# Layer 2's product table in a four-layer graph network: one fp32r pass over stacked parts in place of fp32 matmuls

## The reference, cut to what matters

```python
h = h + segment_sum(basis[:, s, None] * x_j, row * 25 + idx[:, s], n * 25)   # s in 0..3
out = einsum('nki,kio->no', h.reshape(n, 25, 32), weight)
out = out / clip(deg, 1.0)[:, None]
out = out + x @ root_weight + bias
```

## Time and profile before

| what | value |
|---|---|
| median of 3 runs | 12156.67 us (12153.4 to 12159.37) |
| the profiled execution's own time | 12152.8 us |
| its span in the profile | 12150.8 us |
| mean granted TensorE clock over the span | 0.954 |
| stretch in which the table is made | 2984.58 us (first transpose) to 3170.68 us (first gather from Y) |

### The profile page before, as it was taken

How to read it: one execution, slowest core, us unless ns; L and a number is a source line. 1 busy time by engine, 2 the same in 40 slices (tenths; PEclk the granted TensorE clock), 3 DMA queues, 4 the chain that set the end, 5 groups by cost and what they waited for, 6 DMA issues and landing times. The chain is left out here.

```text
span 12150.8 us, 162337 instructions
## 1 busy us (share of the span) xinstructions
PE 11232.7 (92%) x60501; PEld 10209.6 (84%) x60501; DVE 8232.4 (68%) x11388; ACT 6704.3 (55%) x6601; POOL 8276.5 (68%) x8260
## 2 busy tenths in 40 slices
PE   4999668897899999998999899989999899989997
PEld 3999657776699999997888788878888788878886
DVE  4777647776588888886666566665666566656666
ACT  1434234443688888885555455554555455545554
POOL 3777666665466666664777677767777677767776
PEclk9999889998799999998999899998999899989998
DMA  6333132222333333331222222222222222222222
GB/s 194 98 94 97 53 55 72 66 64 69 104 85 87 85 87 86 86 87 49 85 84 90 66 79 87 87 79 65 90 84 86 59 89 86 84 62 86 86 84 68
DMA packets 589302, 1002.20 MB, mean 82 GB/s; under 512 B 172415, under 2 KB 431228, under 8 KB 570220
## 3 DMA queue, kind: packets, MB, share of 16 engines
q1 hardware_dynamic: 284075, 704.29, 16.2%
q0 software_dynamic: 288992, 294.48, 12.1%
q10 hardware_dynamic: 15936, 0.65, 0.1%
HBM read 622.32 MB, written 418.90 MB: 86 GB/s over the span
## 5 line engine op out<-in xcount | busy, mean ns | idle before, releaser
L1957 POOL DMA_INDIRECT l3g<-TQ,srcs x4480 | 4463.5, 996 | 1647.9 <-issue 1029.4
L2075 PE MATMUL ps<-qs,oh 128*128 128x384 f32 (+1 forms) x26880 | 5539.3, 359 | 0.0
L2075 PEld LDWEIGHTS ps<-qs,oh 128*128 128x128 f32 x26880 | 4877.2, 190 | 76.9
L2239 DVE TENSOR_REDUCE l3g<-ps 128x32 f32<-128x416 f32 x3360 | 1917.8, 584 | 2040.1 <-PE ps L2075 2022.5
L2162 ACT CAST oh<-nd 128x1536 fp32r<-128x1536 bf16 x1120 | 1653.7, 1477 | 1732.3 <-DVE nd L2235 1732.3
L1826 PE MATMUL ps<-l2mm,l2oh 128*128 128x408 f32 (+1 forms) x12544 | 2390.5, 352 | 24.4 <-DVE l2mm L1898 24.4
L1826 PEld LDWEIGHTS ps<-l2mm,l2oh 128*128 128x128 f32 x12544 | 2332.8, 188 | 64.8 <-DVE l2mm L1898 25.2
L1810 POOL DMA_INDIRECT l2g<-Y,place x1568 | 1598.5, 1019 | 917.9 <-DVE l2mm L1898 395.4
L1898 DVE TENSOR_TENSOR l2mm<-l2hl,psv 128x1768 fp32r<-128x1768 f32 x784 | 1532.2, 1992 | 261.8 <-PE ps L1826 257.8
L1841 ACT ACTIVATE l2oh<-l2far,l2one 128x512 fp32r<-128x512 f16 x1568 | 1135.2, 724 | 293.3 <-PE ps L1826 290.9
L1023 POOL DMA_INDIRECT l0g<-T,srcs x896 | 967.8, 1080 | 442.1 <-issue 227.8
(11 more groups left out here) (352 smaller groups left out, 9015.7 us busy)
## 6 DMA issues: line engine op xcount, KB each, us to landing
W<-l3o SPq DMA_DIRECT2D x140, 1792.0 KB, 5.8
mneg<-KG SPq DMA_DIRECT2D x280, 384.0 KB, 3.4
l3g<-TQ,srcs POOLq DMA_INDIRECT x4480
l3t<-AT SPq DMA_DIRECT2D x140, 448.0 KB, 3.9
W<-l1o SPq DMA_DIRECT2D x28, 952.0 KB, 4.4
l0e<-U_a SPq DMA_DIRECT2D x28, 896.0 KB, 4.6
S<-RX SPq DMA_DIRECT2D x49, 512.0 KB, 5.0
W<-l0e SPq DMA_DIRECT2D x28, 896.0 KB, 3.7
```

The costliest lines, as they stand in the source:

```text
L1957: e.indirect_dma_start(G3[s][:, j, :], None, TQ, bass.IndirectOffsetOnAxis(ap=srcs[:, c * C + j:c * C + j + 1], axis=0)).then_inc(z3[f"g{s ...
L2075: x_ = e.matmul(ps[k % 3][:, 0:32 * n], OH[k // SB][:, g, 128 * (k % SB):128 * (k % SB) + 128], QS[:, p, 32 * n0:32 * (n0 + n)], start=Fal ...
L2239: e.tensor_reduce(G3[r // KP % 3][:, C - KP + r % KP, :], ps[r % KP % 3][:, 0:32 * PH].rearrange("p (h f) -> p f h", f=32), AXX, ALU.max). ...
```

## The change

Each number is split in two parts: `hi`, its value rounded to fp32r, and `lo`, what is left. A product x*w is then the sum of four products of parts. The features of a node are laid out as (hi, lo, hi, lo), 4 x 32 = 128 numbers, and the matrices on 128 partitions as (hi, hi, lo, lo), so that one fp32r matmul with a contraction of 128 rows sums all four. The root matrix becomes columns 800 to 831 of the same tile. `weights2_v` and `parts2_v` are new work of DVE; the weight and the root matrix are each loaded four times, to four groups of 32 partitions. The tiles live in buffers of layer 1 that are free by then: XT2 in `qs1`, the matrices W2 in `l1oh`, the features' parts XS in `l1g`.

```diff
-            w2s = sb(ph, "w2s", [32, 25, 32])
-            rt = sb(ph, "rt", [32, 32])
+            w2s = sb(ph, "w2s", [128, 832])
...
-            XT2 = [S1f[0:32, 896 * i:896 * i + 896] for i in range(2)]
+            XT2 = [QS1[:, i, 0:896] for i in range(2)]
+            W2 = OH1[0][:, 0, 0:832]
+            W2H = OH1[1][64:128, 0, 0:832]
...
-            e.dma_start(w2s[:, :, :], w2.rearrange("k i o -> i k o")).then_inc(z2["w"], 16)
-            e.dma_start(rt[:, :], root2).then_inc(z2["w"], 16)
+            for b in range(4):
+                rows = slice(32 * b, 32 * b + 32)
+                e.dma_start(w2s[rows, 0:800].rearrange("i (k o) -> i k o", o=32),
+                            w2.rearrange("k i o -> i k o")).then_inc(z2["w"], 16)
+                e.dma_start(w2s[rows, 800:832], root2).then_inc(z2["w"], 16)
...
-            e.wait_ge(*z2.at("w", 48))
+            e.wait_ge(*z2.at("wp", 1))
...
-            e.wait_ge(z1["sq"], NGR + g + 1)
+            e.wait_ge(*z2.at("xp", g + 1))
...
-                x_ = e.transpose(ps[c // 4][0:32, 128 * (c % 4):128 * (c % 4) + 128], X[:, GR * g + c, :], ident[:, :])
+                x_ = e.transpose(ps[c // 4][:, 128 * (c % 4):128 * (c % 4) + 128],
+                                 XS[g % 2][:, c, :, :].rearrange("p k f -> p (k f)"), ident[:, :])
...
-                    e.matmul(ps[2 + n % 4][:, 0:400], xt[:, 128 * c:128 * c + 128],
-                             w2s[:, :, :].rearrange("i k o -> i (k o)")[:, 400 * h:400 * h + 400],
+                    e.matmul(ps[2 + n % 4][:, 0:400], xt[:, 128 * c:128 * c + 128], W2[:, 400 * h:400 * h + 400],
                              start=True, stop=True).then_inc(z2["mm"], 1)
...
-                x_ = e.matmul(ps[6][:, 32 * c:32 * c + 32], xt[:, 128 * c:128 * c + 128], rt[:, :], start=True, stop=True)
+                x_ = e.matmul(ps[6][:, 32 * c:32 * c + 32], xt[:, 128 * c:128 * c + 128], W2[:, 800:832],
+                              start=True, stop=True)
...
-                e.copy(XT2[g % 2][:, 512 * h:512 * h + 128 * w], ps[h][0:32, 0:128 * w]).then_inc(z2["xts"], 1)
+                e.copy(XT2[g % 2][:, 512 * h:512 * h + 128 * w], ps[h][:, 0:128 * w]).then_inc(z2["xts"], 1)
...
+        def weights2_v(e, vc):
+            e.wait_ge(*z2.at("w", 144))
+            vc.up(e.tensor_copy(W2[0:64, :], w2s[0:64, :]).then_inc(vec, 1))
+            a = vc.up(e.tensor_copy(W2H, w2s[64:128, :]).then_inc(vec, 1))
+            e.wait_ge(vec, a)
+            e.tensor_tensor(W2[64:128, :], w2s[64:128, :], W2H.bitcast(F32), ALU.subtract).then_inc(z2["wp"], 1)
+
+        def parts2_v(e, vc, g):
+            xs, x = XS[g % 2], X[:, GR * g:GR * g + GR, :]
+            if g >= 2:
+                e.wait_ge(*z2.at("xt", 2 * (g - 1)))
+            e.wait_ge(z1["sq"], NGR + g + 1)
+            a = vc.up(e.tensor_copy(xs[:, :, 0, :].bitcast(F32R), x).then_inc(vec, 1))
+            e.wait_ge(vec, a)
+            a = vc.up(e.tensor_tensor(xs[:, :, 1, :], x, xs[:, :, 0, :], ALU.subtract).then_inc(vec, 1))
+            e.wait_ge(vec, a)
+            e.tensor_copy(xs[:, :, 2:4, :], xs[:, :, 0:2, :]).then_inc(z2["xp"], 1)
...
             weights3_v(e, vc)
-            e.wait_ge(*z2.at("w", 48))
+            weights2_v(e, vc)
...
                 layernorm_v(e, vc, nd, X, c0, c1, NGR + g, z1["sq"])
+                parts2_v(e, vc, g)
                 if g:
                     root2_v(e, g - 1)
```

More of the change, by code:

```diff
@@ L314, in program @@
             MAf, S1f = (t_[:, :, :].rearrange("p a b -> p (a b)") for t_ in (MA, S1))
-            XT2 = [S1f[0:32, 896 * i:896 * i + 896] for i in range(2)]
+            XT2 = [QS1[:, i, 0:896] for i in range(2)]
+            W2 = OH1[0][:, 0, 0:832]
+            W2H = OH1[1][64:128, 0, 0:832]
+            XS = [G1[1][:, :, :].rearrange("p a b -> p (a b)")[:, 896 * i:896 * i + 896].rearrange(
+                "p (c k f) -> p c k f", k=4, f=32) for i in range(2)]
             Yb = [t_[:, :, :].rearrange("p a b -> p (a b)")[:, 800 * i:800 * i + 800] for t_ in (G1[0], MA) for i in range(2)]
@@ L384, in program @@
         w3 = Named(sem, "w3", "zero loaded mm made")
-        z2 = Named(sem, "l2", "g0 g1 w xt xts mm evs y0 y1 y2 y3 rmm rx line zero prod hl mk far oh used g2",
+        z2 = Named(sem, "l2", "g0 g1 w xt xts mm evs y0 y1 y2 y3 rmm rx line zero prod hl mk far oh used g2 xp wp",
                    z0.over(g0=16 * (C - KP0) * 14, g1=16 * (C - KP0) * 14, e0=16 * 14, e1=16 * 14, kb0=16 * NCH,
```

## The result

The changed kernel takes 12050.87 us, the median of four runs (12049.28 to 12053.37); the kernel before, run beside it and pooled with the runs shown, takes 12155.76 (12153.4 to 12159.37). The ratio is 0.9914 with a 95% interval of 0.9903 to 0.9925: 104.9 us less, 0.86%. The forecast was 12061, the range 12046 to 12084.

The account below looks back on a forecast made before the run. PE bounds layer 1's tail stage, behind which all engines join. The stage gives back 98.7 us, loads cost 4: 94.7 less makes 12058.1 on the profiled execution, about 12061 measured; range 12046 to 12084.

Parts of the forecast that it names:

- the forecast case: Whole kernel: all terms as chosen, about 12061 us with its own range of 12055 to 12066; chance 50%.
- the clock rival: Layer 1's tail: filled 128-row fp32r matmuls raise the clock from 0.50, saving 6.8 us more, 12054; chance 15%.
- ACT's copies set the pace at 0.386: Layer 1's tail: 400-column products take 0.333 us, so ACT's overlapping copies out of PSUM, 0.386 us each, pace it.
- copies don't overlap: Rival, layer 1's tail: ACT's copies take 0.53 us each, 7 us more in all, 12068; chance 12%.
- it doesn't do what it says: Rival: 128-row fp32r takes the passes of fp32, nothing saved, the loads' 4 us lost, 12161; no gain 2%.
- The period: Each group in layer 1's tail: 7.25 us to DVE's root read plus 4.60 to next products, 11.85 replacing 26.35.
- turn-round of 4.60: Between groups: 4.60 us from DVE's root read through layer norm, square root and copies to the next products.
- The stores: Layer 1's tail: column stores, 1.06 to 1.29 us each, queue within a group, off the path except in the last.
- Stores are the pace: Rival, layer 1's tail: slow stores hold up column buffers or set the period, 12074 to 12084; chance 14%.
- DVE's new work: Layer 1's tail: parts2_v about 1.2 us under 5 us of cover, weights2_v about 2.2 under 2.3; both hidden.
- Gathers held up by DVE: Layer 1's tail: DVE's casts and copies might delay POOL's gather issue by 1.9 us at most; nothing taken.
- The loads: Start of layer 1: six more DMAs prolong ACT's issuing and delay PE's first pick by 4 us, bounds 0 to 5.3.

Follow-up runs that it names:

- e10: Changed kernel with fp32r product and root matmuls on only 32 of the 128 rows, three of four part products left out: 12055.76 us, ratio 0.992.
- e7: Kernel before, with DVE's read of the root products one group later and a second PSUM bank for them: 12142.7 us, ratio 0.999.
- e11: Changed kernel with product and root matmuls in true fp32 on the same stacked 128 rows: 12091.75 us, ratio 0.9948.
- e5: Changed kernel with six buffers for finished columns awaiting their store, in place of four: 12048.51 us.
- e12: Kernel before with the changed kernel's nine matrix loads in place of its three, the added copies not read: 12156.58 us, ratio 1.0002.
- e3: Changed kernel with fp32r matmuls on only 32 of the 128 rows, on a chip where every kernel was slower: 14682.15 us, ratio 0.9948.
- e9: Changed kernel, unchanged, run again as reference in a later round: 12050.36 us, ratio 0.9915 against the kernel before.

## Why the prediction was right, point by point

The range held, the forecast case did not: 12050.9 lies below its 12055 to 12066. The clock (4.1 us of stage), the loads (4 us) and the earlier start of the stage (2.1 us, in no term) all went the same way, and that the measured time is still inside the range is owed to its lower end, which was set for the clock rival with free loads, and in part to luck. The last step of the sum also has a slip: 12058.1 + 3.9 is 12062.0, not 12061.

- **The stage is PE's, all engines meet behind it.** Right. The stage gives 103.6 of the 102.0 us; the earlier start and the longer rest make the difference of 1.6. POOL's first gather came 105.7 us earlier, where about 95 were forecast.
- **A product takes 0.333 us at the low clock, ACT's copies set the pace at 0.386.** Right: 0.33 and 0.385 were measured, the first copy 0.73 us after the first product as forecast. The seven transposes, forecast unchanged, took 1.75 us at the low clock against 1.67. So the rival "copies don't overlap" (0.53) is out, and "it doesn't do what it says" with it.
- **The period: 7.25 us to DVE's read, 4.60 more, 11.85.** Group 0 of the changed kernel took 7.36 and 4.70, 12.06. With the clock held low by the 32-row kernel (e10) the other four are 11.51 to 11.76, the step from group 5 to 6 is 8.79 (forecast 8.85), the end 10.5 (10.7), and the stage 77.93 us against my 78.8. The sum for the low clock was right to 1 us. That the turn-round of 4.60 costs 2.9 us a group more than the 1.69 without it was confirmed apart, by e7.
- **The clock rises: a rival at 15%.** This is the term that I chose wrongly. It rose, as this rival said, though not throughout: it is 0.50 in groups 0 and 3, rises in the course of groups 1, 2, 4 and 5, the mean is 0.68, and the gain is 4.1 us of stage where the rival had 6.8. The argument against it, that PE idles in each period, was half right: the clock was low again at the start of groups 1 to 5. The argument for it, that all 128 rows are filled, is the one that e10 and e11 bear out.
- **The stores.** They queue within a group, as forecast: the landing median went from 2.4 us to 3.2 and the largest to 5.6. At a share of 1.02 they move 398 GB/s, 1.03 us a column (forecast 1.06). In group 0 ACT waited 2.38 us for a buffer, but behind the copies that release the root products, so it did not lengthen the period by that. "Stores are the pace" is out; the waits for free buffers cost some 0.5 us in group 0 and no more than the 2.3 us of stage of e5.
- **DVE's new work.** `parts2_v` takes a cast of 0.39, a subtraction of 0.39 and a copy of 0.42, about 1.3 us with signals (forecast 1.2), and is hidden in the changed kernel. `weights2_v` was expected to fit in 2.3 us of cover. DVE's timeline at the start of the tail shows it just does:

```profile
2975.45 0.12 DVE L1768 TENSOR_SCALAR has<-cnt 128x49 f32<-128x49 f32 x1
2975.61 0.58 DVE L1415 CAST l1oh<-w2s 64x832 fp32r<-64x832 f32 x1
2976.23 0.59 DVE L1416 CAST l1oh<-w2s 64x832 fp32r<-64x832 f32 x1
2976.85 1.02 DVE L1418 TENSOR_TENSOR l1oh<-w2s,l1oh 64x832 fp32r<-64x832 f32 x1
2977.91 0.23 DVE L1697 TENSOR_SCALAR stb<-l1n 128x7 f32<-128x7 f32 x1
...
2986.79 0.17 DVE L1697 TENSOR_SCALAR stb<-l1n 128x7 f32<-128x7 f32 x1 [3.07 <-DMA l1n<-W,lastq]
```

  Three instructions take 2.30 us, and group 0's norm follows without the 2.30 us wait of the earlier trace rows. Group 1's wait shrank from 4.43 to 3.07 us and is still there, so nothing was pushed out.
- **Gathers held up by DVE: nothing taken.** Right in size. Beside the two casts a gather's issue took 0.99 and 1.01 us where 0.94 is usual, some 0.1 us in all and far from 1.9; the tail of the kernel before, without such casts, has single ones of 1.00, 1.09 and 1.10. "SBUF — State Buffer" of the Trainium skill (the section "SBUF: two separate sides") describes this hold-up; this case's trace shows no sure sign of it.
- **The loads: 4 us.** Wrong. I scaled the time of NH's issue by rows of the loads. PE's first pick came 2.6 us earlier than before, not 4 later, and ACT's eight issues took 8.24 us with nine loads in the changed kernel and 8.93 in e12, against 10.53 and 9.29 (e7) with three. So the added rows did not prolong ACT's issuing; why not is not shown.

In numbers, on the profiled executions: I forecast 94.7 and got 102.0. The stage adds 4.9 (4.1 of it the clock), the loads that cost nothing and the earlier start of the stage add 4 + 2.1, and what follows the stage takes 3.7 back: 94.7 + 4.9 + 6.1 - 3.7 = 102.0.

## What to carry to other kernels

When a matmul becomes four times cheaper, the stage falls to the next engine's pitch: here ACT's 0.385 us a copy and the 4.7 us chain from one group's roots over DVE's layer norm to the next products, so the time after is found by writing out that chain, not by scaling the old one. Remove such a chain only with the next supplier in view: the same edit gave 12.6 us on the kernel before (12155.29 - 12142.7) and 7.8 on the changed one, where gathers came due and, in one group, a store. Here matmuls that fill all 128 rows were cheaper than their passes say, because the clock was higher in parts; look at the granted clock of the stretch, and try the rows and the type apart. A range that reaches to the rivals can hold while the chosen case fails, so check each term against the trace.

## What was not expected of the hardware

**In this stage the clock rose only where the matmuls filled 128 rows.** At 32 rows it was 0.50 (1.2 GHz) over the stretches shown of three kernels: fp32 with PE busy 162.63 of 163.13 us (e7), and fp32r with 50.82 of 66 (e3) and 59.74 of 78 (e10). At 128 rows it rose to 1.00 (2.4 GHz) in parts: a mean of 0.89 with fp32 (busy 93.43 of 114) and 0.68 with fp32r (50.96 of 74). It fell back while or after PE stood idle for the next group: in the changed kernel it was 1.00 when group 1's matmuls ended after 3010, and 0.50 when group 2's began at 3014.06, and 1.00 again from 3018. In group 3 it did not rise at all, with 128 rows filled and PE busy from 3024.7 to 3033.4, and it did not in e9 either: filled rows went with the rise, but did not always bring it. "TensorE: Matmul & The Clock Gate" of the Trainium skill (Part 1) says that sustained matmul activity releases the throttle; the 32-row rows do not agree with that if activity is read as busy time. Whether it is the rows or what stands in them, and whether a number between 32 and 128 would do, was not tried.

**One pass of fp32r stands for four of fp32.** A 400-column fp32 product took 1.34 us at 1.2 GHz and 0.67 at 2.4; an fp32r one took 0.33 at 1.2 GHz (starts at 2991.93 and 2992.59, two products apart).
